# Last layer: merging only each tile's last node, with a plain path for all nodes

## The reference, cut to what matters

```
x = _layernorm(x + L0(x))                               # five propagation hops and a projection
k, v = conv(x[src], edge_attr, edge_sh)                 # per edge, 8 heads
alpha  = einsum(q[dst], Wdot, k)
ealpha = exp(alpha - segment_max(alpha, dst)[dst])
attn   = ealpha / segment_sum(ealpha, dst)[dst]
out    = segment_sum(attn * v, dst) @ Wout              # per node
x = _layernorm(x + out)
```

## Time and profile before

| | us |
|---|---|
| median of 3 runs | 4298.92 (4298.04 to 4300.90) |
| the profiled execution, its own time | 4296.22 |
| its span | 4294.4 |

### The profile page before, as it was taken

How to read it: one execution, slowest core, us unless ns; L and a number is a source line. 1 busy time by engine, 2 the same in 40 slices (tenths; PEclk the granted TensorE clock), 3 DMA queues, 4 the chain that set the end, 5 groups by cost and what they waited for, 6 DMA issues and landing times. The chain is left out here.

```text
span 4294.4 us, 73928 instructions
## 1 busy us (share of the span) xinstructions
PE 3850.2 (90%) x26543; PEld 3217.3 (75%) x26543; DVE 2991.5 (70%) x4132; ACT 1983.6 (46%) x2885; POOL 1917.1 (45%) x2002
## 2 busy tenths in 40 slices
PE   4664999999999999964999999999999999999932
PEld 4664999999999999952777777777777777777732
DVE  8996554455444543353888888888888888888845
ACT  5663666556665665521333333333333333333314
POOL 5661000000000000036777777777777777777354
PEclk9886999999999999977999999999999999999965
DMA  6997999999999995515677777777777777777534
GB/s 165 190 190 206 291 290 298 297 293 293 297 296 294 289 294 184 176 47 153 199 220 218 217 218 217 219 215 216 220 212 220 216 216 220 211 221 218 167 124 66
DMA packets 828613, 944.06 MB, mean 220 GB/s; under 512 B 495597, under 2 KB 601849, under 8 KB 828115
## 3 DMA queue, kind: packets, MB, share of 16 engines
q1 hardware_dynamic: 767875, 814.70, 64.4%
q0 software_dynamic: 60368, 124.52, 12.4%
HBM read 648.66 MB, written 289.97 MB: 219 GB/s over the span
## 5 line engine op out<-in xcount | busy, mean ns | idle before, releaser
L2317 POOL DMA_INDIRECT feats_hops<-x_table,src_s x1616 | 1542.3, 954 | 529.5 <-issue 455.5
L1286 PE MATMUL acc<-t_wide,scaled 128*128 128x448 f32 x6860 | 1409.7, 367 | 24.2 <-DVE t_wide L1380 24.2
L1286 PEld LDWEIGHTS acc<-t_wide,scaled 128*128 128x128 f32 x6860 | 1284.8, 188 | 129.5 <-DVE scaled L1398 24.6
L1321 ACT CAST t_wide<-t_ring 128x1568 fp32r<-128x1568 uint8 x490 | 737.7, 1506 | 565.6 <-PE acc L1286 547.7
L1380 DVE CAST t_wide<-t_ring 128x1568 fp32r<-128x1568 uint8 x490 | 478.4, 977 | 734.0 <-PE acc L1286 717.8
L1809 POOL MEMSET l_eps<- 128x1 f32 x1 | 0.1, 103 | 1453.5 <-POOLq L1498 1453.5
L2518 ACT ACTIVATE e_hid_k<-e_turn_ps,e_b 128x512 f32<-128x512 f32 x202 | 139.3, 689 | 593.0 <-PE e_turn_ps L2438 589.6
L2354 PE MATMUL e_turn_ps<-e_weighted,e_spot 128*128 128x128 f32 x3232 | 394.7, 275 | 9.2 <-DVE e_weighted L2582 9.2
L2405 PE MATMUL e_ring_ps<-e_wlin_v,e_x_gv 128*128 128x128 f32 x3232 | 394.0, 275 | 0.4 <-DVE feats_hops L2550 0.4
L2354 PEld LDWEIGHTS e_turn_ps<-e_weighted,e_spot 128*128 128x128 f32 x3232 | 376.8, 192 | 11.2 <-DVE e_weighted L2582 11.2
L2512 ACT COPY e_x_t<-e_turn_ps 128x512 f32<-128x512 f32 x404 | 217.4, 589 | 359.8 <-PE e_turn_ps L2427 358.3
(11 more groups left out here) (275 smaller groups left out, 4885.9 us busy)
## 6 DMA issues: line engine op xcount, KB each, us to landing
t_ring<-adjacency_bytes SPq DMA_DIRECT2D x490, 512.0 KB, 5.7
sums_table<-e_out_rows SPq DMA_DIRECT2D x202, 576.0 KB
q_first<-hop_zeros_q SPq DMA_DIRECT2D x101, 512.0 KB, 5.8
e_sh<-parts_sh SPq DMA_DIRECT2D x404, 128.0 KB
e_ea<-parts_ea SPq DMA_DIRECT2D x404, 128.0 KB
e_q_rows<-q_first SPq DMA_DIRECT2D x202, 256.0 KB, 4.8
e_same<-same_row SPq DMA_DIRECT2D x404, 128.0 KB
adjacency_bytes<-lists_staged SPq DMA_DIRECT2D x196, 256.0 KB, 4.6
```

The lines of the kernel that those rows point to most:

```text
L1286: mm = nc.tensor.matmul(acc[c][:, 0:n], U[p][:, b, :], wide[m % WIDE_RING][:, lo:lo + n], start=(b == 0 and p == 0), stop=(b == NB - 1 and ...
L1321: nc.scalar.copy(into, of).then_inc(wide_act, 1)
L2317: nc.gpsimd.indirect_dma_start(x_rows[i % XR][:, g * GT + t, :], None, x1_table, bass.IndirectOffsetOnAxis(ap=src_ix[:, at:at + 1], axis=0 ...
```

## The change

Every node takes a plain path: its row of `sums_table` (by `row_first`) is divided by its own denominator (`prepare_nodes`), as though no node ran over a tile's end, and goes on through `Wout`, residual and norm. The results are stored as before. For the nodes that do run over a tile's end these rows are not final.

Beside that, the last node of each of the 1616 tiles is handled again, in 13 blocks of 128 (`ends`): its row in the tile is gathered from `sums_table` by `end_row`, merged with the scan's result for what follows (`find_falls`, `find_shares`, `prepare_ends`), and goes through `Wout`, residual (`end_x`, gathered from `x1_table` by `end_ix`) and norm. When all plain rows are stored, 13 scatters write these rows over the finished ones by `end_out`. A tile whose last node does not go on, or did not begin in it, writes to a row of its own behind the result; the output tensor has 1665 such rows more, which are cut off. The table `next_table`, its store, the wait for it and the 49 gathers from it are gone; the scan's result stays in SBUF (`next_rows`).

The work is counted in units of four blocks: 13 units of nodes (0 to 12, the last of one block) and 4 of ends (13 to 16, the last of one block). Gathers have one semaphore per two units. DVE does in step u: prepare unit u, `measure(u - 2)`, `invert(u - 3)`; units 0 and 1 are prepared between the steps of the front; `find_falls`, for all ends at once, stands at the end of step 12 and waits for all gathers of ends. The front has two PSUM banks for each of its names where it had four, so that some turns wait for a copy.

Outside the last layer: `locate_edges` computes `end_row`, `end_ix` and `end_out` in place of `row_next`, on 13 columns, and loads two more small arrays. `fpos` has its columns in the tiles' own order, and the edge pass reads them as two runs of four. The loads of the two rows of edge numbers go into the middle of the edge pass, the comparison (`link`) to its end on DVE, the 13 gathers of `end_x` to its end on POOL; they use memory of `x_res`, which is free by then.

The diff, cut (`measure` and `invert` are as before, by units):

```diff
-            dve.wait_ge(tiles_in, 32)
+            dve.wait_ge(tiles_in, 64)
...
-            chain(nc.vector.tensor_scalar(place[:], first[:], 7, None, ALU.logical_shift_right))
-            chain(nc.vector.tensor_scalar(last[:], last_edge[:], 7, None, ALU.logical_shift_right))
-            chain(nc.vector.tensor_tensor(far[:], last[:], place[:], ALU.is_gt))
-            alone = float(B * P - 1)
-            chain(nc.vector.tensor_scalar(after[:], place[:], 1.0 - alone, None, ALU.add))
-            chain(nc.vector.tensor_tensor(after[:], after[:], far[:], ALU.mult))
-            chain(nc.vector.tensor_scalar(row_next[:], after[:], alone, None, ALU.add))
+
+            tile, behind, pair, sub, base, end, same_end, from_0, crosses, valid, trash, away, node_low, node_high = t_int
+            dve.wait_ge(counted, 2)
+            chain(nc.vector.tensor_scalar(tile[:], tile_i[:], float(G * GT - 1), None, ALU.min))
+            chain(nc.vector.tensor_scalar(behind[:], tile[:], float(N * GT), None, ALU.is_ge))
+            chain(nc.vector.scalar_tensor_tensor(out=tile[:], in0=behind[:], scalar=-float(N * GT), in1=tile[:],
+                                                 op0=ALU.mult, op1=ALU.add))
+            nc.vector.tensor_scalar(pair[:], tile[:], 2, 10, ALU.logical_shift_right, ALU.logical_shift_left)
+            chain(nc.vector.tensor_scalar(sub[:], tile[:], GT - 1, None, ALU.bitwise_and))
+            chain(nc.vector.scalar_tensor_tensor(out=base[:], in0=behind[:], scalar=float(GT), in1=sub[:],
+                                                 op0=ALU.mult, op1=ALU.add))
+            chain(nc.vector.tensor_tensor(base[:], base[:], pair[:], ALU.add))
+            nc.vector.scalar_tensor_tensor(out=end_row[:], in0=spot[:, :, P - 1], scalar=float(2 * GT), in1=base[:],
+                                           op0=ALU.mult, op1=ALU.add)
+            nc.vector.tensor_copy(end[:], tile_dst[:, :, P - 1])
+            nc.vector.tensor_tensor(crosses[:], tile_dst[:, :, P - 1], tile_next[:], ALU.is_equal)
+            chain(nc.vector.tensor_tensor(same_end[:], tile_dst[:, :, P - 1], tile_before[:], ALU.is_equal))
+            chain(nc.vector.scalar_tensor_tensor(out=from_0[:], in0=spot[:, :, P - 1], scalar=0.0, in1=same_end[:],
+                                                 op0=ALU.is_equal, op1=ALU.mult))
+            nc.vector.tensor_tensor(valid[:], crosses[:], from_0[:], ALU.is_gt)
+            chain(nc.vector.tensor_scalar(trash[:], tile_i[:], float(a["n_nodes"] + 1), None, ALU.add))
+            chain(nc.vector.tensor_tensor(away[:], end[:], trash[:], ALU.subtract))
+            chain(nc.vector.tensor_tensor(away[:], away[:], valid[:], ALU.mult))
+            chain(nc.vector.tensor_tensor(end_out[:], away[:], trash[:], ALU.add))
+            nc.vector.tensor_scalar(node_low[:], end[:], P - 1, None, ALU.bitwise_and)
+            chain(nc.vector.tensor_scalar(node_high[:], end[:], 7, None, ALU.logical_shift_right))
+            chain(nc.vector.scalar_tensor_tensor(out=end_ix[:], in0=node_low[:], scalar=float(NB), in1=node_high[:],
+                                                 op0=ALU.mult, op1=ALU.add))
...
+                if i == N // 2:
+                    for into, name in ((link[:, 1:G * GT + 1], "tile_start"), (link_later, "tile_later")):
+                        sp.dma_start(into.bitcast(I32), a[name].to_broadcast([P, G * GT])).then_inc(link_in, 16)
...
+            for b in range(end_x.shape[1]):
+                nc.gpsimd.indirect_dma_start(
+                    end_x[:, b, :], None, x1_table,
+                    bass.IndirectOffsetOnAxis(ap=end_ix[:, b:b + 1], axis=0)).then_inc(end_got, 16)
+            pool.wait_ge(end_got, 16 * end_x.shape[1])
...
-                nc.vector.tensor_copy(score_ps[:, 2 * P:2 * P + K], fpos[:, j * K:(j + 1) * K]).then_inc(v_spot, 1)
+                nc.vector.tensor_copy(score_ps[:, 2 * P:2 * P + K].rearrange("p (g t) -> p g t", g=2), by_pair[:, j]).then_inc(v_spot, 1)
...
+            dve.wait_ge(link_in, 32)
+            nc.vector.tensor_tensor(link[:, 1:G * GT + 1], link[:, 1:G * GT + 1].bitcast(I32), link_later.bitcast(I32),
+                                    ALU.is_equal).then_inc(const, 1)
...
+    NODE_QUADS = [(b, min(4, NB - b)) for b in range(0, NB, 4)]
+    END_QUADS = [(b, min(4, B - b)) for b in range(0, B, 4)]
+    NQ, EQ = len(NODE_QUADS), len(END_QUADS)
+    UNITS = NODE_QUADS + END_QUADS
+    NU = NQ + EQ
...
-        sum_ps = [ctx.enter_context(nc.psum_tensor(f"o_sum_ps{n}", [P, 512], F32)) for n in range(4)]
-        head_ps = [ctx.enter_context(nc.psum_tensor(f"o_head_ps{n}", [P, 512], F32)) for n in range(4)]
...
+        sum_ps, head_ps, f_ps, y_ps = ps("sum_ps"), ps("head_ps"), ps("f_ps"), ps("y_ps")
...
-            sp.dma_start(start[:], a["tile_start"].to_broadcast([P, TILES])).then_inc(start_in, 16)
-            sp.dma_start(later[:], a["tile_later"].to_broadcast([P, TILES])).then_inc(start_in, 16)
...
-            sp.wait_ge(rows_kept, len(quads) + 2)
-            sp.dma_start(next_table.rearrange("(b p) r -> p b r", p=P), next_rows[:]).then_inc(table_out, 16)
...
-            for b in range(NB):
-                nc.gpsimd.indirect_dma_start(
-                    rows[:, b, :], None, sums_table,
-                    bass.IndirectOffsetOnAxis(ap=row_first[:, b:b + 1], axis=0)).then_inc(first_got, 16)
-            pool.wait_ge(table_out, 16)
-            for p, (b0, size) in enumerate(PARTS):
-                for b in range(b0, b0 + size):
+            for u in range(NU):
+                into, _, b0, n = unit(u)
+                index = row_first if u < NQ else end_row
+                for b in range(b0, b0 + n):
                     nc.gpsimd.indirect_dma_start(
-                        more[:, b, :], None, next_table,
-                        bass.IndirectOffsetOnAxis(ap=row_next[:, b:b + 1], axis=0)).then_inc(next_got[p], 16)
+                        into[:, b, :], None, sums_table,
+                        bass.IndirectOffsetOnAxis(ap=index[:, b:b + 1], axis=0)).then_inc(got[part_of[u]], 16)
+            pool.wait_ge(stored, n_stored)
+            for u in range(NQ, NU):
+                b0, n = UNITS[u]
+                pool.wait_ge(normalised, u + 1)
+                for b in range(b0, b0 + n):
+                    nc.gpsimd.indirect_dma_start(
+                        out, bass.IndirectOffsetOnAxis(ap=end_out[:, b:b + 1], axis=0),
+                        end_x[:, b, :], None).then_inc(patched, 16)
+            pool.wait_ge(patched, 16 * B)
...
-            pe.wait_ge(rows_kept, len(quads) + 2)
-            for p in range(NPARTS):
-                pe.wait_ge(merged, p + 1)
...
+            for u in range(NU + 1):
+                if u < NU:
+                    turn(u)
+                if u >= 1:
+                    multiply(u - 1)
+                if u == 1:
+                    pe.wait_ge(scanned, 2)
...
+                if u == 2:
+                    pe.wait_ge(scaled, 1)
+                    for n, (b0, size) in enumerate(END_QUADS):
+                        if n >= 2:
+                            pe.wait_ge(rows_kept, n + 1)
+                        for j in range(size):
+                            tr = nc.tensor.transpose(sum_ps[n % 2][:, j * P:(j + 1) * P],
+                                                     sums[:, 1 + (b0 + j) * P:1 + (b0 + j + 1) * P], ident[:])
+                        tr.then_inc(back, 1)
...
+                if u == NQ - 1:
+                    act.wait_ge(fallen, 1)
+                    nc.scalar.activation(fall[:], fall[:], ACT.Exp).then_inc(exped, 1)
...
+            def prepare_nodes(u):
+                b, n = UNITS[u]
+                at = slice(b, b + n)
+                dve.wait_ge(got[part_of[u]], got_all(part_of[u]))
+                chain(nc.vector.reciprocal(inverse[:, at, :], rows[:, at, D + H:ROW]))
+                chain(nc.vector.tensor_tensor(share[:, at, :], inverse[:, at, :],
+                                              has_edges[:, at].unsqueeze(2).to_broadcast([P, n, H]), ALU.mult))
+                nc.vector.tensor_tensor(rows[:, at, 0:D].rearrange("p b (h c) -> p b h c", h=H),
+                                        rows[:, at, 0:D].rearrange("p b (h c) -> p b h c", h=H),
+                                        share[:, at, :].unsqueeze(3).to_broadcast([P, n, H, D // H]), ALU.mult).then_inc(prepared, 1)
+
+            def find_falls():
+                for p in range(part_of[NQ], len(PARTS)):
+                    dve.wait_ge(got[p], got_all(p))
+                dve.wait_ge(rows_kept, 2)
+                chain(nc.vector.tensor_tensor(peak[:], ends[:, :, D:D + H], next_rows[:, :, D:D + H], ALU.max))
+                nc.vector.tensor_tensor(fall[:, 0, :, :], ends[:, :, D:D + H], peak[:], ALU.subtract)
+                nc.vector.tensor_tensor(fall[:, 1, :, :], next_rows[:, :, D:D + H], peak[:], ALU.subtract).then_inc(fallen, 1)
+
+            def find_shares():
```

(53 more changed lines are left out.)

382 lines of the change are left out of this document (175 added, 207 removed).

## The result

The changed kernel takes 4268.16 us, the median of four runs (4264.13 to 4272.13), against 4299.91 for the kernel before in the same comparison: ratio 0.9926, 95% interval 0.9914 to 0.9938, or 32 us less. I had predicted 4253, 46 us less, with a range that ended at 4268, just under what was measured. The direction and the mechanism of the saving hold; the gain is a third smaller than forecast.

A forecast was written before the change was run, and what follows sets the result against it. Bound: about 95 us of gather issue, then about 80 us of VectorE's merge-and-normalise loop. Last gather's landing 4207.5 + tail 38 + index 3.0 = span 4248.5 against 4294.4; median forecast 4253, range 4242 to 4268.

The forecast's parts named there:

- Index arithmetic: In `locate_edges`: six integer steps go, fourteen chained and six unchained come, two loads added; +3.0 us (1.8 to 4.5).
- Edge pass: Added `end_x` gathers, moved link comparison and loads, and two-run copy all hide in the edge pass: 0 us.
- rival 4: The edge pass gets longer, 4354 if the two-run copy costs 0.5 us in each of 202 pairs; chance 5%.
- The sign that I had set for it: Last layer's first gather more than 10 us late would prove that the edge pass had got longer.
- Up to the last gather: Last layer: 62 gathers in one run, 76.6 us of steps plus 11.3 for the front and 2.0 for the node loop.
- T0: Landing of the last layer's last gather, forecast at 4207.5 in the old time scale.
- rival 1: Shared port slows gathers in every unit of the last layer's node loop, 9.4 us longer: 4262; chance 12%.
- rival 3: Front no longer slows gathers so much, or the tail overlaps better, 10 us less: 4243; chance 10%.
- VectorE's cover: Last layer: VectorE's eleven node units at some 3.6 us end at 4193, leaving 15 us of cover, front's edits cost 0.
- Rival 2: VectorE's loop, at 6.8 us a unit, not GpSimd, sets the last gather's landing time: 4270; chance 8%.
- The tail: From the last gather's landing to the end: merge, remaining units, 13 scatters, landing, 0.8 us program end; 38 us, +-5.
- What was not touched: Propagate and the first layer, whose code is unchanged, were put at 0 us of change.

The follow-up runs named there:

- ends_early: Changed kernel with end rows gathered and merged after three node units, scatters waiting only for node stores, SyncE waiting for their landing: 4268.45 us, ratio 0.9926.
- sp_waits: Changed kernel with the wait for the 13 scatters' landing moved from GpSimd's end to SyncE's: 4264.51 us, ratio 0.9916.
- best: Changed kernel at the old SBUF addresses, SyncE waiting for the scatters' landing, VectorE's first operation held until GpSimd's four memsets are done: 4258.88 us, ratio 0.9906.
- no_scatter: Changed kernel without the 13 scatters and the waits ahead of and behind them: 4248.67 us, ratio 0.9882.

## Why the prediction was off

My forecast lies 15 us below the median. By its own terms: tail +7.2, propagate +3.8, first layer and edge pass +3.5, index stage -0.6, and 1.3 because the profiled execution lies 4.0 under its median instead of 2.7. That is the whole of it, for this pair of profiles.

- **Index arithmetic** (+3.0): measured +2.40. Over all runs the stage takes 30.1 to 30.3 us without the additions and 32.6 to 33.3 with them. Right. (Two sums of the prediction are off by 0.1 us, without effect: its +1.8 comes to +1.9, and 11 x 1.03 to 11.3, not 11.4.)
- **Edge pass** (0): its length is 2156.8 to 2161.1 us over all 14 later profiles of both kernels, without order. Gathers of `end_x`, link loads and the two-run copy are hidden; rival 4 is out. The sign that I had set for it did come: the first gather starts 10.6 us later than before (4125.52 against 4114.94). But only 1.6 of that lie in the edge pass; the sign could not tell this pass from the stages ahead of it.
- **Up to the last gather** (T0 = 93.9 us behind the stage's start): 93.9, to the tenth by luck, since errors cancel. The first gather starts 2.16 us into the stage instead of 1.33, as two memsets beside `apart` took 0.98 and 0.96 us. The gathers' run is 0.8 shorter than my sum: the front slows them by 11.9 us (11.3 in the sum), the node loop by 0.6 (2.0). In the node loop one gather took 1.42 us, the rest 0.99 or less. The Trainium skill's rule on the port pair ("SBUF — State Buffer", section "SBUF: two separate sides") has a VectorE instruction with two inputs in SBUF hold the pair only against a GpSimd operation that reads SBUF. Taken for every unit, as in rival 1, it would have slowed a gather in each; the trace shows gathers slowed beside the front's long scans (4.20 and 3.24 us above) and hardly beside the loop's multiplies. Rival 1 is out, and so is rival 3: the front slows the gathers nearly as much as it did (11.9 us, 12.87 before), and the tail is longer, not shorter.
- **VectorE's cover** (15 us): VectorE stood idle for GpSimd's gathers 14.5 us in all, 8.5 for node rows and 6.0 ahead of `find_falls`. That is close, again with errors that cancel. Units take 4.06 us when nothing is awaited from GpSimd (4204.91 to 4208.97), not 3.6, since the step from `measure` to `normalise` and back was not in my price; but VectorE's loop began 2.6 us sooner in the stage. Rival 2, at 6.8 us a unit, is out. In `ends_early`, where the work on ends went into this cover, the unit's price decided.
- **The tail** (38): this is the step that failed. "With 0.8 us of program end" took the end from a kernel whose last instruction was a SyncE store. Here it is a GpSimd scatter, behind which the queue drains for 6.17 us, so that 7.8 us follow the last issue's end instead of 2.1: 5.7 of the tail's 7.2. The first scatter came 1.4 us late (0.8 of it lies between ACT's last row and the scatter's start); scatters and landing (1.4) were right.
- **What was not touched** (0): the other step that failed, by leaving it out. Propagate's code is the same and its time is not: on average 1455.1 us in four profiles at the old addresses (two kernels), 1459.5 in seven at the new ones (both kernels again). In single profiles the first hop's spread of some 3 us lies over that. The first layer (100.9 to 104.1 us over all profiles) shows no such order; its +1.87 I count as spread, which is argued, not shown.

At the old addresses the changed kernel takes 4258.06 us, 40 less than before. The rest of the gap to the 46 that I had forecast, some 6 us, is as large as what the drain adds.

## What to carry to other kernels

When the last work of a block moves to GpSimd, add the drain of its queue behind the last indirect DMA (4 to 9 us from the issue's end here), and look for it in the rows of the block's own line, in an earlier block of the same kernel if need be. When a change exchanges tiles that stay allocated, look up which later tiles move, and keep their addresses (a dummy tile does it) before a difference of a few microseconds is put down to the change's work. A gather-bound stretch tells nothing of the engine just behind it: price that engine's loop with its waits before anything is reordered.

## What the runs showed of the hardware

- The drain of a GpSimd queue that has issued indirect DMAs ends 6.2 us after the last issue's end where nothing is waited for (`sp_waits`, `ends_early` and `best`, behind scatters), 5.1 in `no_scatter` (behind gathers), 4.15 in the first layer, and 8.1 in the last layer and 8.6 in the edge pass of the kernel before. Behind a wait for the landing it still takes 6.17 us, in both profiles of the changed kernel, and 5.70 at the end of its edge pass. It runs beside other engines' work, and beside landing transfers. What sets its length stays open.
- TensorE's pace on the same matmuls has at least three values (a ring tile in 2.83, 2.84 or 2.89 us), and how often the slow one comes goes by where in SBUF its inputs lie; 32 to 64 bytes moved the whole kernel by up to 15 us (4258.06 to 4273.41). The Trainium skill ("SBUF — State Buffer", section "SBUF: two separate sides") says that on the engine side only VectorE's and GpSimd's shared port pair causes contention, and TensorE waits on nobody. From that I would have expected no price on these places; the measurements show one. Whether TensorE waits for something there or is slower by itself, no run tells.
- The slow pace comes for whole stretches. Of the long stretches near a hop's start, one in each hop behind the first, 16 of 28 had it at -32, 0 of 16 at the old place and 0 of 4 at +32; in the first hop it comes at any of these places.
